# A four-layer kernel: in the steps of layer 0, TensorE's product with the values moved from behind the output product to directly behind the scores

## The reference, cut to what matters

```python
# first half, per sequence and head
q, k, v = fcq(x @ wq), fck(x @ wk), fcv(x @ wv)
x = x + softmax(q @ k.T / 8) @ v @ fco
# second half
light = softmax(window(q @ kk.T)) @ vv @ w_out            # 8 heads, window of 64 with its neighbours
# routing weights: 50 iterations of
a = logk - logsumexp(s + b); b = -relu(s + a)
# then the 128 best queries and 256 best keys per sequence, and
heavy = softmax([null, q_sel @ k_sel.T]) @ [null_v, v_sel] @ w_out_h
x = x + light + scatter(heavy)
```

## Time and profile before

| | before |
|---|---|
| median of 3 runs | 1706.64 us (1705.35 to 1707.17) |
| the profiled execution's own time | 1702.27 us |
| its span | 1700.5 us |
| PE busy | 1498.4 us (88%) |
| DVE busy | 1093.9 us (64%) |
| ACT busy | 931.8 us (55%) |
| POOL busy | 633.1 us (37%) |
| mean granted clock of TensorE | 0.959 of full speed |

### The profile page before, as it was taken

How to read it: one execution, slowest core, us unless ns; L and a number is a source line. 1 busy time by engine, 2 the same in 40 slices (tenths; PEclk the granted TensorE clock), 3 DMA queues, 4 the chain that set the end, 5 groups by cost and what they waited for, 6 DMA issues and landing times. The chain is left out here.

```text
span 1700.5 us, 31052 instructions
## 1 busy us (share of the span) xinstructions
PE 1498.4 (88%) x10612; PEld 1040.2 (61%) x10612; DVE 1093.9 (64%) x2737; ACT 931.8 (55%) x2458; POOL 633.1 (37%) x819
## 2 busy tenths in 40 slices
PE   7999999998999998999999895888789866999976
PEld 5666677666666665777877663555457623555643
DVE  5588888775666663655554445777523277899964
ACT  3577788555555563544454441334344347878945
POOL 2798878710010001002220252323424401888820
PEclk8999999999999998999999997999989977999999
DMA  8000000000000003000000124000012121333300
GB/s 278 1 2 1 2 1 16 11 1 1 1 1 1 1 2 116 1 2 17 17 17 23 34 65 165 9 1 11 26 45 61 40 78 34 89 86 87 93 14 25
DMA packets 46215, 62.76 MB, mean 37 GB/s; under 512 B 7832, under 2 KB 32480, under 8 KB 45312
## 3 DMA queue, kind: packets, MB, share of 16 engines
q1 hardware_dynamic: 41520, 51.41, 10.2%
q0 software_dynamic: 4544, 9.38, 1.5%
HBM read 50.21 MB, written 15.75 MB: 39 GB/s over the span
## 5 line engine op out<-in xcount | busy, mean ns | idle before, releaser
L2368 POOL TENSOR_TENSOR weighted<-state,c_all 128x512 f32<-128x512 f32 x128 | 163.6, 1299 | 78.7 <-DVE state L2378 64.9
L926 DVE TENSOR_REDUCE pair_negmax<-psum_all 128x2 f32<-128x512 f32 x192 | 123.4, 684 | 71.8 <-PE psum_all L613 71.5
L754 ACT ACTIVATE probs<-psum_all,pair_shift 128x256 f32<-128x256 f32 x256 | 117.9, 472 | 76.5 <-POOL pair_shift L449 75.9
L2378 DVE TENSOR_TENSOR_SCAN state<-decay,psum_all 128x512 f32<-128x512 f32 x128 | 149.0, 1200 | 14.3 <-PE psum_all L2296 11.5
L754 ACT ACTIVATE probs<-psum_all,pair_negmax 128x256 f32<-128x256 f32 x192 | 88.5, 473 | 106.3 <-DVE pair_negmax L926 60.2
L2005 POOL DMA_INDIRECT found<-values,dest x78 | 74.9, 960 | 153.4 <-ACT values L1998 129.1
L449 POOL TENSOR_SCALAR pair_shift<-pair_negmax,row_term 128x1 f32<-128x1 f32 x256 | 102.8, 419 | 76.9 <-DVE pair_negmax L926 76.4
L456 POOL TENSOR_SCALAR probs<-probs,pair_recip 128x256 f32<-128x256 f32 x128 | 122.9, 967 | 8.3 <-DVE pair_recip L946 8.2
L765 ACT ACTIVATE probsT<-psum_all 128x512 f32<-128x512 f32 x224 | 122.5, 612 | 0.3 <-PE psum_all L626 0.3
L2306 PE MATMUL psum_all<-weighted,ident 128*128 128x512 f32 x256 | 121.7, 600 | 0.0
L626 PE MATMUL psum_all<-ident,probs 128*128 128x128 f32 x896 | 117.1, 274 | 0.1
(11 more groups left out here) (403 smaller groups left out, 3465.5 us busy)
## 6 DMA issues: line engine op xcount, KB each, us to landing
c_all<-c_rows SPq DMA_DIRECT2D x64, 256.0 KB, 3.3
slots<-slot_fill_dram SPq DMA_DIRECT2D x2, 2535.0 KB, 14.2
ring<-slots SPq DMA_DIRECT2D x18, 260.0 KB, 3.1
keys<-found SPq DMA_DIRECT2D x16, 256.0 KB, 4.5
up<-up_dram SPq DMA_DIRECT2D x1, 2048.0 KB, 7.6
down<-down_dram SPq DMA_DIRECT2D x1, 2048.0 KB, 12.1
up<-up_dram SPq DMA_DIRECT2D x1, 1408.0 KB, 5.8
found<-values,dest POOLq DMA_INDIRECT x78, 2.2
```

The source lines that it names most:

```text
L754: nc.scalar.activation(k.probs[:, 2 * (u % PAIR_BUF) + j, t, :], k.psum[score_bank(u, j)][:, SEQ * t:SEQ * (t + 1)], ACT.Exp, bias=shift[: ...
L926: nc.vector.reduce_max(k.pair_negmax[:, u % 2, SUB * j:SUB * (j + 1)], src, AXX, negate=True).then_inc(s.negmax_ready, 1)
L2368: nc.gpsimd.tensor_tensor(w.weighted[:, u % RING, :], w.state[:, u % RING, :], w.c_all[:, u // L3_DC % C_RING, :], ALU.mult)\
L2378: nc.vector.tensor_tensor_scan(w.state[:, u % RING, :], w.decay[:, u % L3_RING, :, :].rearrange("p b n -> p (b n)"), k.psum[u % PARTS_RING ...
```

## The change

One call moves by a few lines in TensorE's loop of layer 0:

```diff
@@ -688,6 +688,8 @@
                 for u in steps:
                     if u < U:
                         scores(u)
+                    if 0 <= u - V_AFTER < U:
+                        weigh_values(u - V_AFTER)
                     for job in early[u]:
                         do(job)
                     if 0 <= u - T_AFTER < U:
@@ -697,8 +699,6 @@
                             scatter(g)
                     if 0 <= u - O_AFTER < U:
                         add_to_output(u - O_AFTER)
-                    if 0 <= u - V_AFTER < U:
-                        weigh_values(u - V_AFTER)
                     for job in late[u]:
                         do(job)
```

## The result

The change makes the kernel slower, by more than forecast: **1748.4 us** (median of 4 runs, 1742.9 to 1752.7) against 1706.0 before (4 runs), ratio **1.0264 (95% interval 1.0223 to 1.0305)**. The forecast was 1734, with a range to 1743. The profiled execution took 1745.6 us.

A forecast was written before the change was run, and what follows sets the result against it. TensorE's own order was taken to bound layer 0's saturated steps, where an early product would wait for ScalarE's and VectorE's copies. 9.3 + 4.3 + 2.0 + 4.0 + 7.8 = 27.4 us on the 1706.6 us median gives 1734 us, range 1718 to 1743.

The forecast's parts named there:

- ahead of unit 8: Steps 4 to 7, ahead of the 32 steps, three of them plain: +2.0 us.
- 32 steps: Layer 0, 74.84 to 224.54 us: new waits of 15.0 us, overlapped by 10.7 us of earlier lost time, +4.3 us.
- 19 steps: Layer 0, 224.54 to 304.87 us, TensorE saturated: 4 steps at +0.7, 15 at +0.51, less 1.2 us, +9.3 us.
- ranking: Steps in which VectorE ranks, 304.87 to 336 us: three at +0.8, a fourth at +1.6, together +4.0 us.
- second half: 16 steps with a heavy projection: it ends later, so L884 is late by 0.49 us each; +7.8 us.
- both bounds of the plain step: Plain main steps of 4.03 us: ScalarE's copies alone give 4.36 (+0.33), VectorE's loop through L982 gives 4.54 (+0.51).
- The rival with ScalarE alone (1723 us): Only ScalarE's copies bind, VectorE keeps up: +0.33 a plain step, 16 us in all; chance 0.25.
- I take about the same behind `values`: Saturated stretch: the product's start of 1.80 us, from the step behind `keys`, assumed behind `values`; 4 such steps at +0.7.
- W: The place in a step, in us behind the scores' start, at which the product starts; forecast 1.58 in plain steps.
- The lock: Rival: VectorE's scaling blocked for a whole GpSimd piece, L982 0.8 later in 54 steps: +43, 1777 us; chance 0.04.
- The rival at 1747 us: The ranking and the second half lose more, +10 to +16 us on top of the forecast; chance 0.08.
- "Faster": Rival: the product fills idle time ahead of the projection and waits nowhere itself, 10 us less, 1697 us; chance 0.05.

The follow-up runs named there:

- Experiment 3: Changed kernel with VectorE's copy of the product out of its bank (L982) done one step earlier, behind the projection's copy; ratio 1.0175 to the kernel before.
- experiment 2: Changed kernel with VectorE's addition of a finished output (L846) moved behind the reciprocal and scaling; ratio 1.0141 to the kernel before.
- experiment 5: Changed kernel with one dummy 128x512 matmul behind the scores of the six steps behind `values` in units 8 to 58; ratio 1.0226 to the kernel before.
- experiment 9: The changed kernel itself, run again on another chip; ratio 1.0234 to the kernel before.
- Experiment 4: Changed kernel with the product directly behind the scores for the 64 main units only, other units as before the change; ratio 1.0188 to the kernel before.
- experiment 7: Kernel before the change, with the product directly behind the scores only in the 8 steps behind a late job `norm_turn`; ratio 0.9972.
- experiment 1: Changed kernel with the early jobs (projection) ahead of the product with values again; ratio 1.0121 to the kernel before.
- experiment 6: Changed kernel with the product moved behind the transposes and ahead of the output product, all steps; ratio 1.0125 to the kernel before.

## Why the prediction was right in direction and too small

By its own terms, in us of the profiled executions:

| term | forecast | measured |
|---|---|---|
| ahead of unit 8 | +2.0 | +0.5 |
| 32 steps | +4.3 | +13.4 |
| 19 steps | +9.3 | +12.9 |
| ranking | +4.0 | +7.5 |
| second half | +7.8 | +9.9 |
| behind layer 0 | 0 | -0.9 |
| sum | +27.4 | +43.3 |

Steps 4 to 7, for which the first term was meant, took 0.8 us more (20.44 against 19.67), with one wait of the product in them; the rest of that row lies ahead of them, where both traces run partly at a lower clock.

- **Right: when the product can start, and both bounds of the plain step.** 4.59 against 4.54. Experiment 3 took VectorE's bound away and found ScalarE's at 4.50. The rival with ScalarE alone (1723 us) is refuted for the changed kernel: there TensorE's product waits 31.1 us for L982 and 7.7 for L765. It is what is left once VectorE's copies are out of the way.
- **Wrong, and the cause of the miss: "I take about the same behind `values`"** (W of 1.80). The value was measured behind `keys` (there W came to 2.00 and 1.85), and carried over. The step ahead of it has L846 in it, once a group, which waits for an instruction that the change makes the last but for the late job. W was 2.94. The prediction says that the output product becomes late too, but prices only the projection's reader and not that of the output product; it comes 1.0 us and the product's wait later. With L846 out of the way (experiment 2) W is 1.83, the 32 steps are at +4.2 and the 19 at +9.5, against 4.3 and 9.3 forecast, and the kernel lies at 1.0141, 24 us, near the 27 of the forecast.
- **Not in the prediction: the clock.** I took 2.4 GHz for granted where TensorE had been saturated. Of the 13.0 us of these six steps, 6.4 go with it (experiment 5). Which of the waits is followed by a slow stretch is in part another from one execution to the next.
- Where the miss lies: the 13.0 us are in the 32 steps (9.2; experiment 2 has 153.9 there) and in the 19 (3.5; 89.8). They cover the misses of 9.1 and 3.6. In the ranking, the step of 10.64 us at a clock of 0.68 is of the same kind (its product waits 2.8 us for L982, behind one more L846 with 0.83 us of wait); with the addition moved, the ranking's five steps took 3.0 us less (35.65 against 38.61). That is +4.5, near the 4.0 forecast, but not as forecast: in the first of them the product starts at 2.90 with or without the addition, where I had 1.91. L982 stands there behind the first ranking of tokens, which the late projection makes late as well, and I had left it at 1.44.
- **Second half**: the mechanism (L884 late, TensorE's next job with it) held in the last ten heavy steps, with +0.42 each where 0.49 was forecast; that is 4.2 us and not 16 times as much. Of the six before them three didn't change (-0.03, -0.02, +0.05), one is +0.96 with L846 waiting 0.56 us in it (+0.31 in experiment 2), and the last two are +1.04 and +2.04, the second of them 9.98 us at a clock of 0.83. Steps without a heavy projection, which I had at nothing, went both ways: five are 0.42 shorter, the second of the half is 1.12 longer, and the first 1.21 shorter, because it ran partly at a lower clock in the kernel before. So the +7.8 is near the +9.9 here, and near the +6.6 of the changed kernel's second trace (experiment 9), partly by luck. Single slow steps make 3 us of difference between these two traces, and the kernel before has one more (8.06 for 6.43). Experiment 4 gives the +9.9 back.
- **The lock** didn't come. In the main steps of the changed kernel L952 overlaps GpSimd's scaling in nearly every one and takes 0.84 us, never more: its second piece takes 0.57 instead of 0.35, and GpSimd's first piece 1.10 instead of 0.95. The Trainium skill's page SBUF — State Buffer (two separate sides) would have the loser, the one that starts second, blocked for the other's whole instruction, if VectorE's instruction runs in a 2-port mode. No view here says in which mode L952 runs. The measurement decides: a block of VectorE for a whole piece of GpSimd would be 1.0 us or so, and there is none of that length in these traces.
- **The rival at 1747 us** has nearly the measured number, but it put 10 to 16 us more into the ranking and the second half. They missed by 3.5 and 2.1; 12.7 of the miss are in the 32 and the 19 steps.
- **"Faster"** was right on its mechanism in 8 steps and wrong in most others: experiment 7 takes those 8 alone.

What stays open: why a gap of 1.8 us is followed by a slow stretch in one group and not in the next; why the clock falls in the second half of experiment 1 behind waits that are hardly longer than before; and whether the product, taken one unit later, when all its data are long there, could stand in front at no cost. That wasn't tried: by the program, the job `values` of the next group but one would overwrite what the product still reads where the second half begins.

## What to carry to other kernels

When an instruction moves forward in one engine's order, list every other instruction that thereby moves back, and for each its reader on the other engines, in rare steps too: here the costly one appears once in eight. A reader that stands ahead of a loop's own work in its queue passes its wait on to the whole loop. And use a filler only where it is ready: in the eight steps behind a late copy the same move wins 5 us, while it costs 0.56 us in a plain step and 0.42 in a late heavy one.

## What the runs showed of the hardware that wasn't expected

- The same groups of matmuls, without any wait, take 4.03, 4.18 or 4.22 us a step by their order alone (old; experiment 1; experiment 6). In experiment 1 the 0.15 are 0.10 more from projection to product than from projection to transposes, and 0.05 more from transposes to output product; in experiment 6 the product starts 0.97 us behind the transposes' start (the output product 0.88 in the old order), and the scores 0.65 behind the output product's (the product 0.54).
- A single wait of 1.8 us in an otherwise busy TensorE is followed in some instances by matmuls at half rate (transposes 1.91 us for 1.04, granted clock 0.79 over the step), in others not (6.33 us, 1.00). One matmul of 1.13 us placed in that gap, which itself still left 0.30 and 0.37 us of waiting, left no slow stretch in any of the six steps of its profile.
